# The setup's weight sums four to nine slots up, the second chunk's front a slot on, and the third chunk's residual through TensorE, in an adaLN block with a selective scan

## The reference

```python
h = _layernorm(x, axis=-1) * (1 + ca) + sa
x = x + ga * _L0_attn_ref(h, A_log, D_param, x_proj_w, dt_proj_w, dt_proj_b)
h = _layernorm(x, axis=-1) * (1 + cb) + sb
x = x + gb * _L0_ffn_ref(h, gate_w, up_w, down_w, gate_s, up_s, down_s)
# the mixer, for each token t and each of 16 states n:
dA = jnp.exp(dt_t[..., None] * A[None])
h = dA * h + dt_t[..., None] * B_t[:, None, :] * x_t[..., None]
y_t = jnp.einsum('bdn,bn->bd', h, C_t) + D_param * x_t
```

## Time and profile before

| | us |
|---|---|
| median of 3 runs | 297.58 (296.85 to 300.57) |
| the profiled execution | 298.21 |
| its span | 296.4 |
| VectorE busy | 265.8 |
| TensorE busy | 250.3 |
| GpSimd busy | 230.1 |
| ScalarE busy | 189.0 |

### The profile page before, as it was taken

How to read it: one execution, slowest core, us unless ns; L and a number is a source line. 1 busy time by engine, 2 the same in 40 slices (tenths; PEclk the granted TensorE clock), 3 DMA queues, 4 the chain that set the end, 5 groups by cost and what they waited for, 6 DMA issues and landing times.

```text
span 296.4 us, 3940 instructions
## 1 busy us (share of the span) xinstructions
PE 250.3 (84%) x1266; PEld 189.8 (64%) x1266; DVE 265.8 (90%) x346; ACT 189.0 (64%) x310; POOL 230.1 (78%) x115
## 2 busy tenths in 40 slices
PE   7876189979997997786499999974799997999993
PEld 7624076668886555564386767752678776787762
DVE  4699998799979989999999899989999999987751
ACT  2376655885656696798646976794357498444650
POOL 1117998989999999998999998699869999960000
PEclk9995558995558799998979999999599997999999
DMA  6915984349546575469152762592776730001102
GB/s 236 370 54 160 133 213 128 100 82 241 125 91 103 86 142 100 90 97 143 34 122 66 152 162 67 113 146 48 146 177 207 150 130 0 2 0 35 38 0 75
DMA packets 34437, 33.81 MB, mean 114 GB/s; under 512 B 14960, under 2 KB 21488, under 8 KB 34416
## 3 DMA queue, kind: packets, MB, share of 16 engines
q1 hardware_dynamic: 34000, 32.73, 49.7%
q10 hardware_dynamic: 416, 0.81, 0.7%
HBM read 31.12 MB, written 2.36 MB: 113 GB/s over the span
## 4 chain that ended last, share of the span: by engine, by line
POOL 29%; PE 29%; DVE 19%; issue 13%; ACT 7%; POOLq 1%; DVEq 0%; ACTq 0%
POOL drv L749 18%; POOL drv L761 10%; DVE state L1223 8%; PE sums L1645 6%; DVE drv L1188 5%; PE side L1367 3%; PE side L1563 2%; PE side L1452 2%; ACT decay L997 2%; PE sums L1614 2%; PE side L1579 2%; PE rows_ps L1602 2%; PE side L1522 2%; PE decay L1356 2%; DVE delta L1114 1%
## 5 line engine op out<-in xcount | busy, mean ns | idle before, releaser
L749 POOL TENSOR_TENSOR drv<-u,brow 128x1024 f32<-128x1024 f32 x63 | 147.7, 2366 | 8.2 <-DVE u L1122 8.1
L997 ACT ACTIVATE decay<-delta,A 128x512 f32<-128x512 f32 x128 | 87.5, 687 | 64.1 <-DVE state L1223 61.6
L1223 DVE TENSOR_TENSOR_SCAN state<-decay,last,drv 128x512 f32<-128x512 f32 x96 | 118.6, 1269 | 3.7 <-ACT decay L997 3.3
L1645 PE MATMUL sums<-ident,drv 128*128 128x128 f32 x504 | 75.3, 304 | 0.5 <-POOL drv L761 0.5
L1645 PEld LDWEIGHTS sums<-ident,drv 128*128 128x128 f32 x504 | 67.0, 160 | 10.4 <-issue 6.3
L761 POOL TENSOR_TENSOR drv<-state,crow 128x1024 f32<-128x1024 f32 x29 | 68.5, 2372 | 5.2 <-DVE state L1223 4.7
L1188 DVE TENSOR_TENSOR drv<-state,rows_ps 128x1024 f32<-128x1024 f32 x34 | 40.7, 1197 | 2.0 <-PE rows_ps L1602 2.0
L1602 PE MATMUL rows_ps<-c_parts,sel 64*128 64x512 f32 x35 | 19.9, 568 | 25.1 <-DVE drv L1188 25.1
L1223 DVE TENSOR_TENSOR_SCAN state<-decay,drv 128x512 f32<-128x512 f32 x32 | 37.6, 1208 | 2.9 <-ACT decay L997 2.8
L1522 PE MATMUL side<-h_hi,ffn_hi 128*128 128x512 f32 x74 | 26.0, 434 | 5.7 <-ACT gates L966 2.4
L1602 PEld LDWEIGHTS rows_ps<-c_parts,sel 64*128 64x128 f32 x35 | 7.3, 208 | 33.9 <-DVE drv L1188 23.1
(11 more groups left out here) (193 smaller groups left out, 346.7 us busy)
## 6 DMA issues: line engine op xcount, KB each, us to landing
brow<-bc_dram SPq DMA_DIRECT2D x31, 512.0 KB, 5.5
crow<-bc_dram SPq DMA_DIRECT2D x13, 512.0 KB, 6.4
resid<-in_x SPq DMA_DIRECT2D x4, 512.0 KB, 5.3
out<-resid SPq DMA_DIRECT2D x8, 256.0 KB, 3.1
gates<-in_wmod ACTq DMA_DIRECT2D x1, 768.0 KB, 6.0
gates<-in_wmod SPq DMA_DIRECT2D x1, 768.0 KB, 7.5
last<-state SPq DMA_DIRECT2D x48, 1.0 KB, 2.6
crow<-bc_dram SPq DMA_DIRECT2D x3, 256.0 KB, 3.5
```

The source lines that it names most:

```text
L749: nc.gpsimd.tensor_tensor(drv[j % RING_DRV][:, :, 0:S], u[:, c % 2, :, 0:S], b.unsqueeze(1).to_broadcast([P, HALVES, S]), ALU.mult).then_i ...
L997: nc.scalar.activation(decay[i % RING_DECAY][:, 0:S], delta[:, c % 2, h, 0:S], ACT.Exp, scale=A[:, h * N + n:h * N + n + 1]).then_inc(deca ...
L1223: nc.vector.tensor_tensor_scan(state[j % RING_STATE][:, h, 0:S], decay[i % RING_DECAY][:, 0:S], drv[j % RING_DRV][:, h, 0:S], before, ALU. ...
L1645: ins = nc.tensor.matmul(sums[:, b * D + h * P:b * D + (h + 1) * P], of[:, h, b * P:(b + 1) * P], ident[:, :], is_transpose=True, start=Fa ...
```

## The change

It changes the tables and one condition. In step 0, TensorE's six parts of `wb` go from slots 10 to 15 to slots 1 to 3, and VectorE takes the sums in slot 3.5 instead of 16; they lie in bank 2 instead of 1, and two of the comparisons and `col` use bank 1. The second chunk's `xT`, `hmod`, `z`, `exp` go one slot on, `abs` and `zb` one and a half. The roundings go one slot up, the comparisons 0.5 to 2 slots on. For the third chunk TensorE adds the residual too, `x2` is ScalarE's copy in slot 2 of step 3 where it was VectorE's addition in slot 1.5, and its norm goes half a slot to a slot on.

```diff
--- before.py
+++ after.py
@@ -84,12 +84,13 @@
 }
 
 
-SECOND_LATER = {"st0": -7, "st1": -7, "agg": 3, "rstd": 2.5, "nmr": 3}
+SECOND_LATER = {"st0": -7, "st1": -7, "agg": 3, "rstd": 2.5, "nmr": 3, "xT": 3, "hmod0": 3, "hmod1": 3, "z": 3,
+                "abs0": 3.5, "zb0": 3.5, "abs1": 3.5, "zb1": 3.5, "exp0": 3, "exp1": 3}
 FIRST = {
     "vector": [
         (0, "F st0"), (0, "F st1"), (0, "F agg"), (0, "F xn1"), (1, "S xpT"), (4, "S mod"), (4, "S W"), (5, "S diag"),
         (6, "S equal0"), (6, "S equal1"), (7, "F clo"), (8, "F delta0"), (8, "F u0"), (8, "F drive0"), (9, "F delta1"), (9, "F u1"),
-        (9, "F drive1"), (17, "S equal2"), (16.5, "S mod2"), (17.5, "S gb"), (31, "S same"), (32, "S wb"),
+        (9, "F drive1"), (17, "S equal2"), (16.5, "S mod2"), (17.5, "S gb"), (19.5, "S wb"), (31, "S same"),
     ],
     "gpsimd": [
         (0, "F nmr"), (3, "S hi0"), (3, "S hi1"), (28, "S down"),
@@ -97,16 +98,16 @@
     "scalar": [
         (0, "F rstd"), (0, "F xn0"), (3, "F hmod0"), (3, "F hmod1"),
         (4, "F abs0"), (4, "F exp0"), (4, "F zb0"), (5, "F bc"), (5, "F chi"), (6, "F ln0"), (6, "F abs1"), (6, "F exp1"), (7, "F zb1"), (7, "F ln1"),
-        (16.5, "S same0"), (17.5, "S same1"), (18.5, "S same2"), (22.5, "S round0"), (23, "S round1"),
-        (23.5, "S round2"), (24, "S round3"), (25.5, "S eq0"), (26.5, "S eq1"), (27.5, "S eq2"),
-        (29.5, "S col"), (30, "S down0"), (30.5, "S down1"),
+        (16.5, "S same0"), (17.5, "S same1"), (18.5, "S same2"), (21.5, "S round0"), (22, "S round1"),
+        (22.5, "S round2"), (23, "S round3"), (26.5, "S eq0"), (28, "S eq1"), (28.5, "S eq2"), (30.5, "S col"),
+        (30, "S down0"), (31, "S down1"),
         (31, "S down2"), (31.5, "S down3"), (32, "S down4"), (33, "S down5"),
     ],
     "tensor": [
         (0, "S warm"), (0, "S warm"), (0, "S mod"), (0, "S xpT"), (1, "F xT"), (1, "S W"),
         (2, "F z0"), (2, "F bc"), (3, "F z1"), (5, "F sp"), (5, "S brow"), (16, "S mod2"), (17, "S gb"),
-        (24, "S eq0"), (25, "S eq1"), (26, "S eq2"), (28, "S col"), (30, "S same"),
-        (26, "S wb0"), (27, "S wb1"), (28, "S wb2"), (29, "S wb3"), (30, "S wb4"), (31, "S wb5"),
+        (25, "S eq0"), (27, "S eq1"), (27, "S eq2"), (29, "S col"), (30, "S same"),
+        (17, "S wb0"), (17, "S wb1"), (18, "S wb2"), (18, "S wb3"), (19, "S wb4"), (19, "S wb5"),
     ],
     "sync": [
         (1, "S x"), (1, "S ffn"), (1, "S wmod"), (6, "F bc"), (18, "S down"), (26, "S xs"),
@@ -131,19 +132,19 @@
 
 CLOSING = {
     "vector": [
-        (1.5, "K x2"), (1.5, "K st0"), (2, "K st1"), (2, "K agg"), (5.5, "K lo0"), (6, "K lo1"),
+        (2, "K st0"), (2.5, "K st1"), (2.5, "K agg"), (6, "K lo0"), (6.5, "K lo1"),
         (10.5, "K hdn5"), (10.5, "K hdn0"), (10.5, "K hdn1"), (11.5, "K hdn2"), (12, "K hdn3"), (12.5, "K hdn4"),
         (18, "K out0"), (19.5, "K out1"),
     ],
     "gpsimd": [
-        (3, "K nmr"),
+        (4, "K nmr"),
     ],
     "scalar": [
-        (3, "K rstd"), (3.5, "K xn0"), (4, "K xn1"), (5, "K hi0"), (5.5, "K hi1"), (7.5, "K gate0"), (7.5, "K gate1"),
+        (2, "K x2"), (3.5, "K rstd"), (4.5, "K xn0"), (5, "K xn1"), (6, "K hi0"), (6, "K hi1"), (7.5, "K gate0"), (7.5, "K gate1"),
         (8.5, "K gate2"), (8.5, "K gate3"), (9, "K gate4"), (9.5, "K mixed"), (10.5, "K silu"),
     ],
     "tensor": [
-        (4, "K h2T"), (6, "K gate0"), (6, "K gate1"), (7, "K gate2"), (7, "K gate3"), (8, "K gate4"), (8, "K mixed"),
+        (5, "K h2T"), (6, "K gate0"), (6, "K gate1"), (7, "K gate2"), (7, "K gate3"), (8, "K gate4"), (8, "K mixed"),
         (9, "K up0"), (10, "K up1"), (11, "K up2"), (11, "K up3"), (12, "K up4"),
         (14, "K down0"), (17, "K down2"),
     ],
@@ -197,7 +198,7 @@
     "F xT": (2, 0), "F z": (2, 0), "F bc": 1, "F sp": (2, 2), "K h2T": (2, 0),
     "K gate0": 0, "K gate1": 1, "K gate2": 0, "K gate3": 1, "K gate4": 0, "K mixed": 2,
     "K up0": 1, "K up1": 0, "K up2": 2, "K up3": 1, "K up4": 0, "K down": (1, 1),
-    "S xpT": 2, "S W": 2, "S brow": 2, "S mod2": 0, "S gb": 1, "S wb": 1, "S same": 0, "S eq0": 0, "S eq1": 0, "S eq2": 0, "S col": 0,
+    "S xpT": 2, "S W": 2, "S brow": 2, "S mod2": 0, "S gb": 1, "S wb": 2, "S same": 0, "S eq0": 0, "S eq1": 1, "S eq2": 0, "S col": 1,
 }
 PLACE_CLOSING = {
     "K h2T": (0, 2), "K gate0": 0, "K gate1": 2, "K gate2": 1, "K gate3": 0, "K gate4": 2, "K mixed": 1,
@@ -1634,7 +1635,7 @@
                                 ins.then_inc(half_added, 1)
                     ins.then_inc(added, 1)
                     return
-                if c < NCH - 2 and 4 <= n < 4 + NBLK[c]:
+                if c < NCH - 1 and 4 <= n < 4 + NBLK[c]:
 
                     b = n - 4
                     pe.wait_ge(x_loaded[c], 16)
```

## The result

| | kernel before | changed kernel |
|---|---|---|
| median of 20 runs, us | 297.67 (294.35 to 300.86) | 299.1 (296.48 to 301.44) |
| the profiled execution, us | 298.21 | 299.08 |
| its span, us | 296.4 | 297.3 |
| mean granted clock of TensorE | 0.883 | 0.882 |

The ratio is 1.0059 with a 95% interval of 1.0032 to 1.0086, so the change costs 1 to 2.6 us, where 3.25 us of gain were forecast.

A forecast was written before the change was run, and what follows sets the result against it. VectorE, busy 90% of the span, was taken to set the pace. The terms 2.0 + 0.6 + 1.05 - 0.1 - 0.3 gave a gain of 3.25 us, so 294.3 us, with a range from 292.0 to 297.6.

The forecast's parts named there:

- `wb` moved, 2.0 + 0.6 us: Step 0: VectorE's two waits for TensorE's rows go (2.0 us); its small `wb` instructions hide in a decay stall (0.6 us).
- a gain of 2.3 us instead of 3.2: The `wb` matmuls priced by the skill's rule, 25 ns each: 44 take 1.1 us, leaving some 0.9 us of late row.
- Second chunk's front later, 1.05 us: Step 0: VectorE's decay stalls shrink, with a new 1.1 us stall at number 6; net gain 1.05 us.
- two lasting terms: Step 0: 0.6 us from VectorE's small `wb` instructions and 1.05 us from the second chunk's later front.
- the first part: The prediction's opening account of what bounds the kernel: VectorE sets the pace, GpSimd is second with lateness mostly hidden.
- The third residual on TensorE: Step 2, slots 7 to 10: four more matmuls, 1.8 us on TensorE, make one row just late; cost 0.1 us.
- The closing part, -0.3: Step 3: the 1.2 us VectorE saves by ScalarE's copy is spent waiting for TensorE, and 0.3 us more is lost.
- `nmr` later in step 3: GpSimd's 2.38 us of standing at the third chunk's `nmr` goes; VectorE gains nothing by itself.
- the slower one: Rival: TensorE stays at the low clock through the second chunk's z in step 0; 1.7 us lost, 299.3 us; chance 0.08.

The follow-up runs named there:

- experiment 2: The kernel before with only the third chunk's part of the change (residual added by TensorE, `x2` copied by ScalarE, norm later); 0.56% slower than before.
- experiment 4: The changed kernel with the third chunk's part undone and GpSimd's `nmr` of a chunk's second norm a slot earlier; ratio to before 0.9973.
- experiments 3 to 6: Four kernels with second-norm `nmr` a slot earlier: the changed kernel; that without the third chunk's part; that with early third-chunk norm (0.9976); the kernel before (0.9957).
- experiments 8 and 10: Third residual on TensorE, early norm, `nmr` earlier in step 1 alone; first with, second without the moves of `wb` and second chunk's front; ratios 0.9968, 0.9962.
- experiment 9: The first of experiments 8 and 10 with the transposes `xT` at slot 0, ahead of the 24 additions; 0.3 us of the removed stall reached the end.

## Why the prediction was wrong, point by point

1. *`wb` moved, 2.0 + 0.6 us.* The mechanism was right for the execution I had: rows waits to zero. But the 2.0 us were read from one execution, whose clock had fallen early; none of the five other profiles with the same setup code has such a wait. The rule of the Trainium skill (VectorE: DVE Perf Modes, section on the TRN2 errata) that would have made the sum a gain of 2.3 us instead of 3.2 has no support here: by it eight of these instructions would take an estimated 0.2 us, and at the high clock too they took 0.95 (TensorE in experiment 2):

```profile
67.58 0.95 PE L1367 MATMUL side<-mod,ffn_sb 128*128 128x1 f32 x8
```

2. *Second chunk's front later, 1.05 us.* Right to 0.3: a stall of 0.98 for 1.1; scan (0,7,1), counted from (0,1,1), 1.34 us sooner, where 1.26 was forecast. Against profiles of before with the same clock the setup part is 1.0 to 1.95 us ahead at (1,0,1); 1.65 was the forecast of its two lasting terms.
3. *The step that failed* is a sentence on GpSimd in the first part: "Its `drive` runs three scans' numbers ahead of the scan that uses it, so its lateness is mostly hidden.". That holds for the drives, not for `nmr`, which stands in the same queue, has no lead, and has decays behind its reader. In the changed kernel GpSimd had no break from 46 us until it had done `nmr` at 103.5, so anything that VectorE won in the rest of step 0 could only turn into waiting there. In the first profile of before the earlier loss hid this wait (0.43 us at that scan); the second shows it at 2.27. It is not the whole: of the lead of 4.2 us at (1,0,1), 3.3 are left at (1,5,1) without this wait, and 1.74 at the end (experiment 4).
4. *The third residual on TensorE* in step 2, -0.1: right in kind; from (1,5,1) to (2,9,0) nothing is lost.
5. *The closing part, -0.3*: the mechanism, waits for TensorE at `out` and for h_lo, was named (1.3 to 1.6 us forecast; 0.55, 0.61 and 0.96 measured at `out0`, `out1` and h_lo), but the sum was mis-sized: 1.5 us of cost instead of 0.3. Of the waits named, the kernel before has 0.55 too, at `out1`, so 1.57 are new. I followed VectorE only to number 6; the late h_hi then also holds a decay (0.41), and another comes late behind the gates (0.66), where I had written that ScalarE's slack takes them up. The new waits together, 2.64, less the 1.22 us of addition spared, give 1.42.
6. *`nmr` later in step 3*: its wait went, and brought nothing, as said.

No rival named this course; the slower one came near the time, 299.3, by a clock that didn't stay low at z. So three terms of the sum fell: the 2.0 us of `wb` (the waits of one execution), what the setup part had won besides (cut off at `nmr`), and the closing part, 1.5 us instead of 0.3. The pieces as measured, about nothing for the setup part and 1.5 us for the closing part, fit the 1 to 2.6 us of the whole. Still open is what decides TensorE's clock at the start of step 2, and why experiments 3 to 6 give back 1.0 to 1.3 us of their lead between (1,5,1) and (2,9,0): in all four the additions there took 5.22 to 5.38 us, against 4.50 in the first profile of before, which fits, but no run set the clock by itself.

## What to carry over

Before pricing a gain on the engine that sets the pace, look in every in-order queue for the small operation without a lead whose reader has the pacing engine's work behind it; where such an engine is busy without a break, an upstream gain ends there. Take a wait for a gain only if a second execution shows it too. When a producer moves half a slot later, follow all of its readers to the point where the times meet again, not just to the first.

## What was not expected of the hardware

The granted clock of TensorE at one place of one program differs between executions: 0.67 and 1.00 in the window 64 to 72 us of the kernel before, and 2.84 to 5.38 us for the same 24 additions at the start of step 2. In the three profiles of experiments 8 and 10 with 2.84 us, TensorE had been idle 2.65 to 2.72 us before the row ahead of them; in all others but experiment 9, whose order there differs, 3.02 to 3.38 us, and the additions took 4.07 to 5.38. The longer idle time and the lower clock go together; the idle time comes first and ends with a product of VectorE, but no run changed it by itself. Two profiles of one kernel that differ in the clock there differ by 2.0 us at the end, more than the closing part costs.
